# Two-of-eight experts: result rows stored by choice and token, and read back as plain blocks

## The chip, the cores and the metric

The kernel runs on one core of one Trainium2 chip. TensorE (PE in the rows, with PEld for its weight loads) multiplies, VectorE (DVE), ScalarE (ACT) and GpSimd (POOL) do the rest, and SyncE (SP) issues most of the transfers. The metric is the time of the whole program on the device in microseconds (us), median of several runs; lower is better.

## What is computed

Eight images of 16 x 16 tokens with 192 channels (2048 tokens) go through four layers, each an attention or convolution part and a feed-forward part. The change is at the seam between the third layer's experts and the fourth layer's attention:

```
def _L2_ffn_ref(hidden_states, router_w, w1, w2):
    ...
    probs = jax.nn.softmax(logits, axis=-1)
    topk_probs, topk_idx = jax.lax.top_k(probs, TOP_K)
    ...
    h = jnp.einsum('th,eih->tei', flat, w1)
    h = jax.nn.silu(h)
    outs = jnp.einsum('tei,ehi->teh', h, w2)
    sel = jnp.take_along_axis(outs, topk_idx[:, :, None], axis=1)
    combined = (sel * balanced[..., None]).sum(axis=1)
    ...
    t = t + _L2_ffn_ref(_ln_t(t), L2_ffn_router_w, L2_ffn_w1, L2_ffn_w2)
    t = t + _L3_attn_ref(_ln_t(t), L3_attn_w_qkv, L3_attn_w_proj)
```

Each token is sent to two of eight experts, the two results are weighted and added to the token, and the normalised sum is projected to the queries, keys and values of a full attention within each image.

## The kernel before, in words

The program is a row of stages, each a block in which every engine runs its own instruction list in order, with waits on semaphores between them; all engines meet at the end of a stage. Three stages matter here.

**Routing, `l2r` (function `route` with `top` = 2).** DVE finds each token's two experts and its place in a list of slots sorted by expert and padded to whole tiles of 128: SLOT_TILES = 40 tiles (5120 slots) for 4096 pairs of token and choice. A matrix product of two one-hot tables (OL and OHT) puts the token's number at its slot; an empty slot holds zero. DVE copies that table from PSUM to `token_at` (L2312), copies each token's two slot numbers to `slots` (L2315), and then works out the gates (from L2318 on). Meanwhile SP loads the experts' weights.

**The experts, `l2e` (`experts_any`).** The 40 tiles go in 20 pairs p. Per pair: POOL fetches the tokens' normalised rows from the DRAM buffer `xn` by `token_at` with two indirect transfers of 128 rows (L2428), up to four pairs ahead (RING = 4), waiting only for TensorE to have turned the pair that used the buffer; TensorE turns them (L2441 to L2443); DVE copies them to XT and copies the remaining weight rows of the tile's expert to W1R (L2506); TensorE does the first layer (L2452, L2455); ACT applies SiLU; TensorE turns the result, DVE copies it to HT (L2514), and TensorE does the second layer into `psY` (L2473). DVE copies that to Y (L2520, two buffers), and SP stores Y to the DRAM buffer `ys` in the order of the slots, 192 KB per pair (L2411). The order per slot of the loop is turn hidden of p+1, first layer of p+2, second layer of p, turn tokens of p+3.

**The attention's inputs, `l3p` (`combined_inputs`).** Image i has two tiles of 128 tokens. POOL gathers the two result rows of each token from `ys` by `slots`, four indirect transfers per image (L2734), those of image i+1 ahead of the statistics of image i. DVE adds them to X, weighted by the gates (combine, L2809, four instructions), takes mean and variance (L154, L157), POOL makes RSTD (L161 to L166), DVE normalises into xn (norm, L185), TensorE turns xn (L195), ACT copies it to xT (L203), TensorE multiplies to psQ and psK (L2759) and psV, ACT copies these to QF, KF (L2783) and Vall. Queries and keys are then split into three bf16 pieces: ACT makes the first and second (L255, L271), DVE the differences q_r and k_r (L267) and the third pieces (L279); SP stores them. DVE's order per image i:

```
norm(i + 1)
qp.vector(nc, dve, QF[u][:, :, :], i, u)
kp.vector(nc, dve, KF[u][:, :, :], i, u)
if i + 2 < B:
    combine(i + 2)
qp.third(nc, dve, i, u)
kp.third(nc, dve, i, u)
```

TensorE's order is Q(i), K(i), turn(i+1), V(i). ACT's is QF(i), first Q piece(i), KF(i), xT(i+1), first K piece(i), second Q piece(i), V(i), second K piece(i).

## Time and profile before

| what | value |
|---|---|
| median of 3 runs | 1279.95 us (1279.7 to 1282.09) |
| profiled execution, its own time | 1278.96 us |
| span of its trace, first to last instruction | 1277.1 us |
| mean granted TensorE clock, share of full | 0.885 |
| busy: PE, DVE, ACT, POOL | 82%, 46%, 34%, 22% |
| stage `l2e` in the trace | 735.2 to 901.8 us |
| stage `l3p` in the trace | 901.8 to 986.6 us |

The profiled execution's time is 1.9 us above its span, and 1.0 us below the median. Busy shares are means over the whole program: each stage has its own limit. In the rows, an entry in square brackets is how long the engine had been idle before the instruction and what it was then released by; POOL indirect transfers are called DMA_INDIRECT.

### The profile page before, as it was taken

What the parts mean: (1) busy time and instruction counts of PE and PEld (TensorE: products, weight loads), DVE (VectorE), ACT (ScalarE), POOL (GpSimd) and SP (SyncE); (2) the same over time, 40 slices, a digit from 0 to 9 for tenths busy, and PEclk for the clock granted to TensorE, in tenths of its full rate; (3) what the DMA queues carried; (4) which work ended last, traced back from release to release, by engine and by line L of the source; (5) the groups of instructions that cost most, each with busy time, mean ns of one, the idle gap of its engine ahead of it and who ended that gap; (6) DMA issues with size and microseconds to landing.
All of it is one profiled execution on the core that took longest, in us unless ns stands there. A gap on an engine that the chain in (4) does not pass through costs nothing. (4 is left out here: it accounts for less than half of the span.)

```text
span 1277.1 us, 21213 instructions
## 1 busy us (share of the span) xinstructions
PE 1045.2 (82%) x7522; PEld 794.2 (62%) x7523; DVE 591.8 (46%) x1420; ACT 435.0 (34%) x880; POOL 286.9 (22%) x473
## 2 busy tenths in 40 slices
PE   6795999996998887999898379999376898767890
PEld 5594878874656665787897336666255455465670
DVE  4742655543114555455655634444364677331112
ACT  3653255553323222344440011111054466412330
POOL 5454301102001111000013042220563212103104
PEclk9865999998999998899787589999698999958895
DMA  7444843300112000100003621120244432044534
GB/s 89 120 115 126 188 92 86 93 7 1 38 62 72 16 0 0 50 2 1 1 2 100 180 56 50 49 49 31 59 107 102 129 97 72 3 142 113 148 112 105
DMA packets 118625, 91.41 MB, mean 72 GB/s; under 512 B 33010, under 2 KB 110924, under 8 KB 117900
## 3 DMA queue, kind: packets, MB, share of 16 engines
q1 hardware_dynamic: 106935, 76.31, 23.1%
q0 software_dynamic: 4992, 10.23, 3.7%
q10 hardware_dynamic: 6613, 3.74, 1.1%
q8 instruction: 53, 0.87, 0.3%
q14 instruction: 32, 0.26, 0.1%
HBM read 64.38 MB, written 28.12 MB: 72 GB/s over the span
## 5 line engine op out<-in xcount | busy, mean ns | idle before, releaser
L1227 DVE TENSOR_REDUCE l0a_nmax<-l0a_psS 98x2 f32<-98x392 f32 x96 | 54.2, 566 | 54.1 <-PE l0a_psS L1042 50.1
L871 DVE TENSOR_REDUCE l3a_nmax<-l3a_psS 128x2 f32<-128x512 f32 x96 | 62.0, 686 | 33.7 <-PE l3a_psS L725 33.4
L2428 POOL DMA_INDIRECT l2e_X<-xn,token_at x40 | 38.4, 961 | 128.2 <-PE l2e_psX L2443 74.9
L2493 ACT ACTIVATE l2e_H<-l2e_psH 128x512 f32<-128x512 f32 x40 | 21.7, 595 | 131.2 <-PE l2e_psH L2455 131.2
L827 ACT ACTIVATE l3a_PT<-l3a_psST 128x512 f32<-128x512 f32 x96 | 54.7, 596 | 29.0 <-PE l3a_psST L755 28.4
L2473 PEld LDWEIGHTS l2e_psY<-W2T,l2e_HT 128*128 128x128 f32 x320 | 51.4, 190 | 18.3 <-issue 18.2
L1177 ACT ACTIVATE l0a_PT<-l0a_psST 98x392 f32<-98x392 f32 x96 | 47.2, 497 | 42.2 <-PE l0a_psST L1084 41.9
L2473 PE MATMUL l2e_psY<-W2T,l2e_HT 128*128 x320 | 57.3, 332 | 3.4 <-DVE l2e_HT L2514 2.1
L2452 PE MATMUL l2e_psH<-W1T,l2e_XT 128*128 x80 | 40.9, 635 | 2.8 <-issue 2.0
L2520 DVE COPY l2e_Y<-l2e_psY 128x384 f32<-128x384 f32 x20 | 11.1, 557 | 65.1 <-PE l2e_psY L2473 65.1
L725 PE MATMUL l3a_psS<-l3a_KS,l3a_QS 96*128 96x256 bf16 x192 | 37.3, 275 | 3.9 <-DMA l3a_KS<-kd 2.9
L2640 PE MATMUL l3e_psH<-l3e_XT,expert_W 128*128 128x256 f32 x96 | 30.3, 443 | 8.6 <-DMA expert_b<-in_L_ffn_b 7.3
L755 PE MATMUL l3a_psST<-l3a_QS,l3a_KS 99*128 99x256 bf16 x192 | 36.6, 273 | 0.4 <-ACT l3a_PT L827 0.3
L1403 DVE TENSOR_TENSOR X<-l0m_psY,X 128x384 f32<-128x384 f32 x8 | 4.5, 557 | 66.6 <-PE l0m_psY L1350 66.6
L2734 POOL DMA_INDIRECT l3p_Y<-ys,slots x32 | 31.8, 993 | 10.8 <-issue 10.5
L1350 PE MATMUL l0m_psY<-early,l0m_hT 128*128 128x192 f32 x192 | 32.3, 328 | 2.4 <-ACT l0m_hT L1375 2.4
L1350 PEld LDWEIGHTS l0m_psY<-early,l0m_hT 128*128 128x128 f32 x192 | 31.1, 190 | 3.9 <-ACT l0m_hT L1375 3.9
L1179 ACT ACTIVATE l0a_PT<-l0a_psST 120x360 f32<-120x360 f32 x48 | 22.1, 470 | 31.8 <-PE l0a_psST L1092 29.2
L1230 DVE TENSOR_REDUCE l0a_nmax<-l0a_psS 120x1 f32<-120x312 f32 x48 | 22.8, 479 | 20.6 <-PE l0a_psS L1051 19.0
L2653 PE MATMUL l3e_psY<-expert_W,l3e_HT 128*128 128x192 f32 x192 | 32.0, 327 | 0.0
L1041 PE MATMUL l0a_psS<-l0a_KS,l0a_QS 96*98 96x196 bf16 x144 | 31.8, 259 | 0.0
L2653 PEld LDWEIGHTS l3e_psY<-expert_W,l3e_HT 128*128 128x128 f32 x192 | 31.1, 190 | 0.3 <-issue 0.3
(534 smaller groups left out, 2752.6 us busy)
## 6 DMA issues: line engine op xcount, KB each, us to landing
l3a_QS<-qd SPq DMA_DIRECT2D x72, 64.0 KB, 2.2
l3a_KS<-kd SPq DMA_DIRECT2D x72, 64.0 KB, 2.2
expert_W<-in_L_ffn_w SPq DMA_DIRECT2D x8, 576.0 KB, 4.7
rd<-l0q_r_p SPq DMA_DIRECT2D x24, 168.0 KB
ys<-l2e_Y SPq DMA_DIRECT2D x20, 192.0 KB, 1.9
l0a_QS<-qd SPq DMA_DIRECT2D x54, 64.0 KB
l0a_KS<-kd SPq DMA_DIRECT2D x54, 64.0 KB
W2T<-in_w2t SPq DMA_DIRECT2D x2, 1536.0 KB
```

Source lines behind the costliest of these rows:

```text
L725: mm = nc.tensor.matmul(psS[item % 2][:, t * T:(t + 1) * T], QS[k % ring][0:SR, s, q:q + P], KS[k % ring][0:SR, s, u * T:(u + 1) * T], sta ...
L755: mm = nc.tensor.matmul(psST[item % 2][:, t * T:(t + 1) * T], KS[k % ring][:, s, key:key + P], QS[k % ring][:, s, u * T:(u + 1) * T], star ...
L827: nc.scalar.activation(PT[n % 3][:, s, :], psST[item % 2][:, :], ACT.Exp).then_inc(exp_done, 1)
L871: nc.vector.tensor_reduce(nmax[k % 2][:, TI * u:TI * (u + 1), s], psS[item % 2][:, :].rearrange("p (t k) -> p t k", t=TI), AX.X, ALU.max, ...
L1041: nc.tensor.matmul(o, q_[:, s, q], k_[:, s, keys], start=True, stop=False)
L1177: ex = nc.scalar.activation(PT[n % 3][0:WQ, s, :], psST[item % 2][0:WQ, 0:2 * W0], ACT.Exp)
L1227: mx = nc.vector.tensor_reduce(nmax[k % 2][0:WQ, 2 * j:2 * (j + 1), s], psS[item % 2][0:WQ, 0:2 * W0].rearrange("p (t k) -> p t k", t=2), ...
L1350: mm = nc.tensor.matmul(psY[a][:, t % 2 * C:(t % 2 + 1) * C], hT[p % 2][:, m, t * P:(t + 1) * P], Wd[:, m, :], start=(m == 0), stop=(m == ...
L2428: pool.indirect_dma_start(out=X[p % RING][:, t, :], out_offset=None, in_=G["xn"], in_offset=bass.IndirectOffsetOnAxis(ap=G["token_at"][:, ...
L2452: nc.tensor.matmul(psH[b][t][:, :], XT[b][:, t, :], W1T[:, 0, bass.ds(e * FI, FI)], start=True, stop=False)
L2473: mm = nc.tensor.matmul(psY[:, t * C:(t + 1) * C], HT[b][t][:, mb, :], W2T[:, bass.ds(e * NM + mb, 1), :].rearrange("p a c -> p (a c)"), s ...
L2653: mm = nc.tensor.matmul(psY[b][:, t * C:(t + 1) * C], HT[b][:, m, t * P:(t + 1) * P], W2[b][:, m, :], start=(m == 0), stop=(m == MF - 1))
```

## The change

The experts' results now go to DRAM by choice and token: row k * 2048 + token of `ys` holds the result of token for choice k. To get there the second one-hot table carries token - 2048 for the first choice and token + 1 for the second, so that sign and zero of the summed table tell first choice, second choice and empty slot apart. DVE works `token_at` and a second table `result_of` out of it; empty slots get a row number beyond the buffer. In `l2e` POOL, and no longer SP, stores each tile's rows with an indirect transfer by `result_of`, with a bound above which rows are dropped; a new semaphore `y_free`, raised by POOL once a pair's store has landed, tells DVE that a Y buffer is free. In `l3p` the rows of an image lie together, so SP loads them as 16 plain blocks of 128 x 2 x 192, all issued at the start of the stage; POOL gathers nothing there. In DVE's list for `l3p`, combine(i+2) moves ahead of the split of image i. The one-expert layer's routing uses the same table and gets a shifted copy in the place of the plain one.

```
@@ -2301,7 +2301,7 @@
-                    V.tensor_tensor(OHT[:].rearrange("p (k t) n -> p k t n", k=top), OH[:].rearrange("p (k t) n -> p k t n", k=top), free(token[:, 0:1], [0, top], [1, NT], [0, TILES]), ALU.mult).then_inc(hot_done, 1)
+                    V.tensor_tensor(OHT[:].rearrange("p (k t) n -> p k t n", k=top), OH[:].rearrange("p (k t) n -> p k t n", k=top), free(token[:, 0:1], [NT, top], [1, NT], [0, TILES]), ALU.mult).then_inc(hot_done, 1)
...
             dve.wait_ge(tab_mm, 1)
-            V.tensor_copy(G["token_at"][:, 0:TILES], psTab[:, 0:TILES]).then_inc(slots_done, 1)
+            tab = psTab[:, 0:TILES]
             if top == 2:
-                for k in range(2):
-                    V.tensor_copy(G["slots"][k][:, :], SI[:, k, :]).then_inc(slots_done, 1)
-
+
+                link(V.tensor_scalar(te[:, :], tab, 0.0, -1.0 - B * T, ALU.is_gt, ALU.mult))
+                link(V.tensor_tensor(te[:, :], tab, te[:, :], ALU.add))
+                V.tensor_scalar(G["token_at"][:, :], te[:, :], float(B * T), float(B * T - 1), ALU.add, ALU.min).then_inc(slots_done, 1)
+                link(V.tensor_scalar(late[:, :], tab, 0.0, None, ALU.is_gt))
+                link(V.tensor_scalar(empty[:, :], tab, 0.0, 2.0 * B * T, ALU.is_equal, ALU.mult))
+                link(V.tensor_tensor(empty[:, :], empty[:, :], late[:, :], ALU.subtract))
+                link(V.tensor_tensor(empty[:, :], tab, empty[:, :], ALU.add))
+                V.tensor_scalar(G["result_of"][:, :], empty[:, :], float(B * T), None, ALU.add).then_inc(slots_done, 1)
+            else:
+                V.tensor_scalar(G["token_at"][:, 0:TILES], tab, float(B * T), float(B * T - 1), ALU.add, ALU.min).then_inc(slots_done, 1)
+            if top == 2:
                 dve.wait_ge(imp_mm, 1)
...
@@ -2403,30 +2412,36 @@
 
         @block.sync
         def _(sp):
-            of_pair = lambda buf, p: image_of(buf.rearrange("(j n) c -> j (n c)", n=2 * P), p, 0, [C, P], [P * C, 2], [1, C])
-
-            def store(q, s):
-                p = q * RING + s
-                sp.wait_ge(y_done, p + 3)
-                sp.dma_start(of_pair(G["ys"], p), Y[s % 2][:, :, :]).then_inc(y_out[s % 2], 16)
-
             early.start(sp)
-            for b in range(2):
-                sp.sem_inc(y_out[b], 16)
-            with sp.Fori(0, PAIRS // RING) as q:
-                for s in range(RING):
-                    store(q, s)
             early.finish(sp)
-            for b in range(2):
-                sp.wait_ge(y_out[b], 16 * (PAIRS // 2 + 1))
 
         @block.gpsimd
         def _(pool):
-            for p in range(PAIRS):
+            at = lambda table, k: bass.IndirectOffsetOnAxis(ap=table[:, k:k + 1], axis=0)
+
+            def fetch(p):
                 pool.wait_ge(xt_mm, p + 1)
                 for t in range(2):
-                    pool.indirect_dma_start(out=X[p % RING][:, t, :], out_offset=None, in_=G["xn"],
-                                            in_offset=bass.IndirectOffsetOnAxis(ap=G["token_at"][:, 2 * p + t:2 * p + t + 1], axis=0)).then_inc(x_in[p % RING], 16)
+                    pool.indirect_dma_start(out=X[p % RING][:, t, :], out_offset=None, in_=G["xn"], in_offset=at(G["token_at"], 2 * p + t)).then_inc(x_in[p % RING], 16)
+
+            def put(p):
+                pool.wait_ge(y_done, p + 3)
+                for t in range(2):
+                    pool.indirect_dma_start(out=G["ys"], out_offset=at(G["result_of"], 2 * p + t), in_=Y[p % 2][:, t, :], in_offset=None,
+                                            bounds_check=2 * B * T - 1, oob_is_err=False).then_inc(y_out[p % 2], 16)
+
+            pool.sem_inc(y_free, 2)
+            for p in range(RING):
+                fetch(p)
+            for p in range(PAIRS):
+                if p + RING < PAIRS:
+                    fetch(p + RING)
+                if p:
+                    pool.wait_ge(y_out[(p - 1) % 2], 32 * ((p - 1) // 2 + 1))
+                    pool.sem_inc(y_free, 1)
+                put(p)
+            for b in range(2):
+                pool.wait_ge(y_out[b], 32 * (PAIRS // 2))
 
         @block.tensor
         def _(pe):
@@ -2516,7 +2531,7 @@
             def result_of(q, s):
                 p, b = q * RING + s, s % 2
                 dve.wait_ge(y_mm, p + 3)
-                dve.wait_ge(y_out[b], q * (RING // 2 * 16) + (s // 2 * 16 + 16))
+                dve.wait_ge(y_free, p + 1)
...
-        Y = [[st.sb(f"Y{t}{k}", [P, C]) for k in range(2)] for t in range(NT)]
+        Y = [[st.sb(f"Y{i}{k}", [P, TI, C]) for k in range(2)] for i in range(B)]
...
+            for i in range(B):
+                for k in range(2):
+                    sp.dma_start(Y[i][k][:], rows(G["ys"], (k * B + i) * T * C, [C, P], [P * C, TI], [1, C])).then_inc(y_in[i], 16)
             for i in range(B):
                 for pieces, dst in ((qp, G["qd"]), (kp, G["kd"])):
                     pieces.sync(sp, rows(dst, i // 2 * 3 * C * 2 * T + i % 2 * T, [2 * T, CH], [2 * C * T, 3], [2 * CH * T, 2], [1, T]), i, i % 2)
...
-            def gather(i):
-                for t in range(TI * i, TI * (i + 1)):
-                    for k in range(2):
-                        pool.indirect_dma_start(out=Y[t][k][:, :], out_offset=None, in_=G["ys"],
-                                                in_offset=bass.IndirectOffsetOnAxis(ap=G["slots"][k][:, t:t + 1], axis=0)).then_inc(y_in[t], 16)
-
             stats.init(pool)
-            gather(0)
             for i in range(B):
-                if i + 1 < B:
-                    gather(i + 1)
                 stats.gpsimd(nc, pool, i, i % 2)
...
-                            dve.wait_ge(y_in[t], 32)
+                            dve.wait_ge(y_in[i], 32)
                         else:
                             dve.wait_ge(added, 2 * TI * i + b + 1)
-                        nc.vector.scalar_tensor_tensor(G["X"][:, t, :], Y[t][k][:, :], G["gates"][k][:, t:t + 1], G["X"][:, t, :], ALU.mult, ALU.add).then_inc(added, 1)
+                        nc.vector.scalar_tensor_tensor(G["X"][:, t, :], Y[i][k][:, b, :], G["gates"][k][:, t:t + 1], G["X"][:, t, :], ALU.mult, ALU.add).then_inc(added, 1)
                 stats.vector(nc, dve, i, i % 2, (added, 2 * TI * (i + 1)))
 
             def norm(i):
@@ -2822,10 +2831,10 @@
                 u = i % 2
                 if i + 1 < B:
                     norm(i + 1)
+                if i + 2 < B:
+                    combine(i + 2)
                 qp.vector(nc, dve, QF[u][:, :, :], i, u)
                 kp.vector(nc, dve, KF[u][:, :, :], i, u)
-                if i + 2 < B:
-                    combine(i + 2)
                 qp.third(nc, dve, i, u)
                 kp.third(nc, dve, i, u)
...
-            "token": (np.arange(NT)[None, :] * P + np.arange(P)[:, None]).astype(np.float16), "blockones": head @ head.T,
+            "token": np.concatenate([np.arange(NT)[None, :] * P + np.arange(P)[:, None] + n for n in (-B * T, 1)], 1).astype(np.float16), "blockones": head @ head.T,
...
+        G["result_of"] = alloc("result_of", SLOT_TILES, U32)
-        slots = SLOT_TILES * P
-        G["ys"] = nc.dram_tensor("ys2", [slots, C], F32).ap()
+        G["ys"] = nc.dram_tensor("ys2", [2 * B * T, C], F32).ap()
```

On DVE at the end of the routing stage, the list around the copy of the slot table, before (te, late and empty are scratch rows of 40 numbers; imp begins the gates):

```order
L2310 CAST tile_expert<-l2r_te 128x40
L2312 CAST token_at<-l2r_psTab 128x40
L2315 CAST slots<-l2r_SI 128x16 x2
L2318 TENSOR_REDUCE l2r_imp<-l2r_psI 128x8
L2319 TENSOR_SCALAR l2r_bal<-l2r_imp 128x8
```

and now:

```order
L2310 CAST tile_expert<-l2r_te 128x40
L2315 TENSOR_SCALAR l2r_te<-l2r_psTab 128x40
L2316 TENSOR_TENSOR l2r_te<-l2r_psTab,l2r_te 128x40
L2317 TENSOR_SCALAR token_at<-l2r_te 128x40
L2318 TENSOR_SCALAR l2r_late<-l2r_psTab 128x40
L2319 TENSOR_SCALAR l2r_empty<-l2r_psTab 128x40
L2320 TENSOR_TENSOR l2r_empty<-l2r_empty,l2r_late 128x40
L2321 TENSOR_TENSOR l2r_empty<-l2r_psTab,l2r_empty 128x40
L2322 TENSOR_SCALAR result_of<-l2r_empty 128x40
L2327 TENSOR_REDUCE l2r_imp<-l2r_psI 128x8
```

Where three copies stood, eight instructions stand, seven of which depend on the one before or read the same table.

On POOL in the experts' stage, one piece of the difference (L2428 and L2425 fetch, L2430 stores):

```order
-L2428 DMA l2e_X<-xn,token_at 128x192 x40
+L2425 DMA l2e_X<-xn,token_at 128x192 x10
+L2430 DMA ys<-l2e_Y,result_of 4096x192 x2
+L2425 DMA l2e_X<-xn,token_at 128x192 x2
+L2430 DMA ys<-l2e_Y,result_of 4096x192 x2
+L2425 DMA l2e_X<-xn,token_at 128x192 x2
```

The forty fetches were one run ahead of the work; now five pairs are fetched first, and then the two stores of a pair stand between the fetches.

On DVE in the stage of the attention's inputs, one image of the loop before, from its norm on (l3p_xn is norm; l3p_q_r and l3p_k_r the differences; l3p_q_p and l3p_k_p the third pieces; X is combine, with its statistics behind it):

```order
L185 TENSOR_SCALAR l3p_xn<-X,MEAN,RSTD 128x192 x2
L267 TENSOR_TENSOR l3p_q_r<-l3p_QF,l3p_q_p 96x512
L267 TENSOR_TENSOR l3p_k_r<-l3p_KF,l3p_k_p 96x512
L2809 SCALAR_TENSOR_TENSOR X<-l3p_Y,gate,X 128x192 x4
L154 BN_STATS l3p_stat_part<-X 128x6 x2
L157 BN_AGGR l3p_stat_mv<-l3p_stat_part 128x2 x2
L279 TENSOR_TENSOR l3p_q_p<-l3p_q_r,l3p_q_p 96x512
L279 TENSOR_TENSOR l3p_k_p<-l3p_k_r,l3p_k_p 96x512
```

and the same image now:

```order
L185 TENSOR_SCALAR l3p_xn<-X,MEAN,RSTD 128x192 x2
L2818 SCALAR_TENSOR_TENSOR X<-l3p_Y,gate,X 128x192 x4
L154 BN_STATS l3p_stat_part<-X 128x6 x2
L157 BN_AGGR l3p_stat_mv<-l3p_stat_part 128x2 x2
L267 TENSOR_TENSOR l3p_q_r<-l3p_QF,l3p_q_p 96x512
L267 TENSOR_TENSOR l3p_k_r<-l3p_KF,l3p_k_p 96x512
L279 TENSOR_TENSOR l3p_q_p<-l3p_q_r,l3p_q_p 96x512
L279 TENSOR_TENSOR l3p_k_p<-l3p_k_r,l3p_k_p 96x512
```

Combine and its statistics now stand right behind norm, ahead of everything that waits for ACT.

## Rows read from the trace of the kernel before

**Rows 1.** Windows: busy PE, PEld, DVE, ACT, POOL, then clock, DMA share, GB/s.

```profile
735.20:901.80 166.60, 152.57 (x740) 99.24 (x740) 66.28 (x120) 22.99 (x41) 38.44 (x40) 0.97 0.18 48
901.80:916.25 14.45, 0.00 (x0) 0.00 (x0) 7.31 (x18) 0.00 (x0) 10.61 (x15) 0.50 0.20 57
933.11:973.25 40.14, 30.35 (x140) 23.79 (x140) 26.65 (x71) 21.48 (x40) 25.25 (x36) 0.91 0.45 114
```

**Rows 2.** Who waited for whom, 690 to 1000 us: total, times, longest.

```profile
PEld l2e_psH L2455 <- DVE l2e_W1R L2506: 13.0, 17, 0.8
```

**Rows 3.** Timeline and one window, end of routing: start, length, engine, line, operation.

```profile
729.86 0.18 DVE L2310 CAST tile_expert<-l2r_te 128x40 int32<-128x40 f32 x1
730.07 0.20 DVE L2312 CAST token_at<-l2r_psTab 128x40 uint32<-128x40 f32 x1
730.34 0.28 DVE L2318 TENSOR_REDUCE l2r_imp<-l2r_psI 128x8 f32<-128x128 f32 x1
724.00:726.00 2.00, 0.00 (x0) 0.00 (x0) 2.00 (x2) 0.00 (x0) 0.00 (x0) 0.50 0.00 0
```

**Rows 4.** Timeline, two slots of the experts' loop, with and without a fetch.

```profile
853.42 0.56 DVE L2520 COPY l2e_Y<-l2e_psY 128x384 f32<-128x384 f32 x1 [3.31 <-PE l2e_psY L2473]
...
855.49 0.95 POOL L2428 DMA_INDIRECT l2e_X<-xn,token_at  x1 [0.30 <-issue]
...
856.07 0.60 DVE L2506 COPY l2e_W1R<-W1T 64x512 f32 x1 [0.64 <-issue]
...
876.34 0.56 DVE L2520 COPY l2e_Y<-l2e_psY 128x384 f32<-128x384 f32 x1 [3.17 <-PE l2e_psY L2473]
...
878.88 0.42 DVE L2506 COPY l2e_W1R<-W1T 64x512 f32 x1 [0.47 <-issue]
```

**Rows 5.** Stores L2411, median us to landing; tile l2e_X, its fetches L2428.

```profile
ys<-l2e_Y SPq DMA_DIRECT2D x20, 192.0 KB, 1.9
...
DMA to landing us min/median/max: 2.5/2.7/4.2
```

**Rows 6.** Timeline, from the experts' last copies to the first norm.

```profile
894.92 0.56 DVE L2520 COPY l2e_Y<-l2e_psY 128x384 f32<-128x384 f32 x1 [1.82 <-PE l2e_psY L2473]
...
898.53 0.56 DVE L2520 COPY l2e_Y<-l2e_psY 128x384 f32<-128x384 f32 x1 [3.06 <-PE l2e_psY L2473]
901.88 0.10 POOL L148 MEMSET l3p_stat_exponent<- 128x2 f32 x1 [45.45 <-POOLq L77]
...
902.62 2.46 DVE L2817 MEMSET Vall<- 128x2880 f32 x1 [0.53 <-issue]
...
916.25 0.80 DVE L185 TENSOR_SCALAR l3p_xn<-X,MEAN,RSTD 128x192 f32<-128x192 f32 x2
```

**Rows 7.** Timeline, first image: its k_r, and the norm of image 2.

```profile
927.64 0.69 DVE L267 TENSOR_TENSOR l3p_k_r<-l3p_KF,l3p_k_p 96x512 f32<-96x512 f32 x1 [2.88 <-ACT l3p_k_p L255]
...
933.11 0.69 DVE L185 TENSOR_SCALAR l3p_xn<-X,MEAN,RSTD 128x192 f32<-128x192 f32 x2 [1.09 <-POOL RSTD L166]
```

**Rows 8.** Timeline, one later image, norm to norm.

```profile
949.17 0.69 DVE L185 TENSOR_SCALAR l3p_xn<-X,MEAN,RSTD 128x192 f32<-128x192 f32 x2 [1.09 <-POOL RSTD L166]
949.78 0.68 DVE L267 TENSOR_TENSOR l3p_q_r<-l3p_QF,l3p_q_p 96x512 f32<-96x512 f32 x1
951.73 0.69 DVE L267 TENSOR_TENSOR l3p_k_r<-l3p_KF,l3p_k_p 96x512 f32<-96x512 f32 x1 [1.28 <-ACT l3p_k_p L255]
952.34 1.39 DVE L2809 SCALAR_TENSOR_TENSOR X<-l3p_Y,gate,X 128x192 f32<-128x192 f32 x4
952.49 0.62 ACT L271 ACTIVATE l3p_k_p<-l3p_k_r 96x512 bf16<-96x512 f32 x1
954.86 0.65 DVE L279 TENSOR_TENSOR l3p_q_p<-l3p_q_r,l3p_q_p 96x512 bf16<-96x512 f32 x1
955.43 0.68 DVE L279 TENSOR_TENSOR l3p_k_p<-l3p_k_r,l3p_k_p 96x512 bf16<-96x512 f32 x1
957.20 0.70 DVE L185 TENSOR_SCALAR l3p_xn<-X,MEAN,RSTD 128x192 f32<-128x192 f32 x2 [1.09 <-POOL RSTD L166]
```

More of the change, by code:

```diff
@@ L2162, in route @@
         over, chosen = st.sb("over", [P, E, NT]), st.sb("chosen", [P, E, E])
-        te, te_cmp = small("te", SLOT_TILES), st.sb("te_cmp", [P, SLOT_TILES, E])
+        te, late, empty, te_cmp = small("te", SLOT_TILES), small("late", SLOT_TILES), small("empty", SLOT_TILES), st.sb("te_cmp", [P, SLOT_TILES, E])
         OH, OHT = (st.sb(n, [P, top * NT, TILES], F16) for n in ("OH", "OHT"))
@@ L2394, in experts_any @@
         y_out = [st.sem(f"y_out{b}") for b in range(2)]
-        xt_mm, xt_done, w_done, h_mm, h_done, ht_mm, ht_done, y_mm, y_done = st.sems("xt_mm xt_done w_done h_mm h_done ht_mm ht_done y_mm y_done")
+        xt_mm, xt_done, w_done, h_mm, h_done, ht_mm, ht_done, y_mm, y_done, y_free = st.sems("xt_mm xt_done w_done h_mm h_done ht_mm ht_done y_mm y_done y_free")
         early = Early(st, transfers)
@@ L2716, in combined_inputs @@
         psV = [st.ps(f"psV{u}") for u in range(2)]
-        y_in = [st.sem(f"y_in{t}") for t in range(NT)]
+        y_in = [st.sem(f"y_in{i}") for i in range(B)]
         added, pads_done, q_mm, q_free, k_mm, k_free, v_free = st.sems("added pads_done q_mm q_free k_mm k_free v_free")
@@ L2933, in __init__ @@
         self.sb(ctx, X=(P, NT, C), MEAN=(P, NT), RSTD=(P, NT), ident=(P, P), early0=(P, EARLY), early1=(P, EARLY))
-        for name, n, dt in (("tri", P, BF16), ("onesb", P, BF16), ("earlier", NT * E + E, BF16), ("count", P, I32), ("token", NT, F16)):
+        for name, n, dt in (("tri", P, BF16), ("onesb", P, BF16), ("earlier", NT * E + E, BF16), ("count", P, I32), ("token", 2 * NT, F16)):
             self.G[name] = ctx.enter_context(nc.sbuf_tensor(name, [P, n], dt))
```

## The prediction

> **What bounds the kernel now.** I read the page first (busy shares, the slices), then busy time by stage, then the list of waits around the change, then the timelines of the three stages. In the experts' stage TensorE works 152.57 us of 166.60 at a granted clock of 0.97 (nearly all at its upper level, 2.4 GHz), and POOL 38.44 [rows 1]: TensorE sets the pace, and what it still waits for is DVE's copy W1R, 17 times for 13.0 us in all [rows 2]. In the 14.45 us before the first norm of the attention's inputs TensorE does nothing at all [rows 1]: everyone waits for gathered rows. In the next stretch no engine is full: over the five images from norm 2 to norm 7, 40.14 us, TensorE has 30.35, DVE 26.65, POOL 25.25 [rows 1]. So one image takes 40.14 / 5 = 8.03 us there, and a loop of waits sets it, not an engine. [rows 8] show the loop: norm at 949.17; ACT must make xT before the first K piece, so k_r starts only at 951.73, after an idle 1.28; combine stands behind k_r and starts at 952.34; POOL's statistics end at 957.20, when the next norm starts after an idle 1.09. The combination, 4.86 us with its statistics (952.34 to 957.20), is in series with norm, turn and K piece.
>
> **The change, part by part.**
>
> Routing. From the copy of the table to the first row of the gates it was 0.27 us (730.07 to 730.34) [rows 3]. Now eight instructions on 128 x 40 stand there. The nearest pitch is that of two linked casts of this shape, 0.21 (729.86 to 730.07) [rows 3], and two of the eight don't wait for the one before: 6 x 0.21 + 2 x 0.15 = 1.6, so 1.3 more. Nothing covers it: no byte moves at 724 to 726 us [rows 3], so the weights are in, and the experts start when DVE is done. **+1.3** (1.0 to 1.6). The shifted copy for the one-expert layer is one instruction for one, 0.
>
> POOL in the experts' loop. The trace has no indirect store and none with a bound. The nearest row is the indirect fetch, 0.95 us and 0.30 between two [rows 4], pitch 1.25. A slot takes (876.34 - 853.42) / 3 = 7.64 us [rows 4], and two stores and two fetches take 5.0 of it: POOL has 2.6 us spare. The fetch of pair p+5 now waits behind the stores of pair p. They start when the copy of p has ended; two stores, two fetches and the landing are 1.25 x 4 + 2.7 [rows 4, 5] = 7.7 us later, and TensorE turns pair p+5 two slots later, at 15.3. So TensorE doesn't wait, and the slack of 7.6 us is the cover: nothing to pay unless a store takes 2.3 us or more. DVE's wait for a free Y (y_free) is for a store two slots old, also covered.
>
> DVE beside POOL. Where the second W1R copy meets a fetch it takes 0.60 in place of 0.42, and it ends 3.25 us after the start of the Y copy in place of 2.96 [rows 4]; as TensorE waits for it [rows 2], the slot is 0.29 longer. Stores and fetches now keep POOL busy for 5 us behind each Y copy, so more slots can meet this: between 0 and 17 x 0.29 = 4.9. Two of the four transfers lie where the fetch lay already, so I take **+1.0**. The Trainium skill, SBUF — State Buffer, section "SBUF: two separate sides", speaks against the change here: it says that a DMA issued from GpSimd needs the port pair that VectorE's fp32 copies within SBUF hold, that whoever comes second is blocked outright, and that issuing from SP avoids it; the copy's 0.60 fits the direction, and what the rule would cost if the whole instruction blocked is the fourth rival.
>
> End of the experts. The last copies start at 894.92 and 898.53 [rows 6] and take 0.56. Before, a plain store landed 1.9 us after issue [rows 5] and the next stage began at 901.88 [rows 6], 2.8 us after the last copy's end. Now the stores of pair 18 go out at about 895.6 and 896.9, and land by 899.6 (2.7, the fetches' median [rows 5]); POOL waits for that before it stores pair 19 at 899.6 and 900.9, which lands at 903.6 in place of some 901.2 (899.1, 0.2 to the issue, 1.9): **+2.4**. With the least plain landing, 1.9, it is +1.0; with the fetches' longest, 4.2 [rows 5], +5.4 (each 0.1 counts twice, as the last two pairs are in series). I take 2.7, as it is the same queue.
>
> Start of the attention's inputs. SP's first two blocks, each as large as a pair's store was, can go out at once and land about 2 us later [rows 5], at 904; DVE's fill of Vall, 902.62 + 2.46 = 905.08 [rows 6], hides them (if they took 1 us more than that, 0.5 would be seen). Then two combines of 2.52 (952.34 to 954.86 [rows 8]) end at 910.1; the first one's statistics are ready 4.86 after its start, at 909.9. The first norm comes at 910.1 in place of 916.25 [rows 6]: **-6.1**.
>
> The first image. From norm 0 to k_r it is 927.64 - 916.25 = 11.4 us [rows 6, 7], a chain through TensorE and ACT at the lower clock (0.50 up to norm 0 [rows 1]), which stays. Before, norm 2 came another 5.5 us later (933.11 [rows 7]), as combine followed k_r. Now combine 2 is over long before; after k_r come ACT's second K piece (0.62) and DVE's third (0.68) [rows 8]: 0.69 + 0.62 + 0.68 and handovers, 2.3 us. **-3.2**.
>
> Five later images. DVE's list is now norm 0.61, combine 2.52, q_r 0.68, k_r 0.69, then the wait for ACT's second K piece 0.62, and the third K piece 0.68 [rows 8]; the third Q piece lies in that wait. That is 5.8, with some 0.3 of handovers 6.1. The first K piece, ready 2.6 us after norm (951.73 against 949.17 [rows 8]), is hidden by combine, and so are the statistics (0.61 + 4.86 = 5.5, under 6.1). TensorE had 30.35 / 5 = 6.07 busy per image at a clock of 0.91 [rows 1], 5.5 at full clock: it fits, narrowly. 8.03 - 6.1 = 1.93 per image, five times: **-9.6** (period 5.6 to 7.0: -12.1 to -5.2). Images 6 and 7 have no combine behind them; from norm 7 on nothing changes.
>
> Sum: 1.3 + 1.0 + 2.4 - 6.1 - 3.2 - 9.6 = -14.2. From the profiled execution's 1278.96 us that gives 1264.8; the median of the runs is 1.0 above that execution, so **1266 us**. Less than 0.2% (2.6 us) can't be told from no change.
>
> **The rivals.**
>
> 1. The stores cost more than fetches: they land after 4.2 us (+5.4) and every slot meets the copy (+4.9): 1.3 + 4.9 + 5.4 - 18.9 = -7.3, 1272.5. For it: rows are written to scattered places, which no row shows. Against: 768 bytes a row before and now. Chance 0.15.
>
> 2. TensorE becomes the bound of the attention's inputs. An image needs 5.5 us of it at full clock, 11 at the 0.50 that it had before the first norm [rows 1]; at a mean of 0.75 the period is 7.4 and the five images give 3.1 in place of 9.6: 1272.5. For it: its share would be 90%. Against: a denser TensorE gave no fall of the clock in the experts' stage (0.97). Chance 0.07.
>
> 3. Slower: POOL becomes the pace of the experts. If a bounded indirect store takes 4 us of POOL, a pair needs 8.6 + 2.5 = 11.1 in place of 7.64, and 17 pairs lose 59 us: 1325. It costs from 2.3 us per store on and makes the whole change a loss from 2.7 (34 stores x 0.4 = 14). For it: nothing here shows a bound's price. Against: the fetch reads a table of row numbers too, and takes 0.95 [rows 4]. Chance 0.06.
>
> 4. W1R is blocked for whole transfers: 17 slots lose up to the 0.95 us of one [rows 4], 16 in place of 1: 1281, no change or slightly slower. This is the rule of the Trainium skill named above taken in full. Against: overlaps in this trace cost 0.29. Chance 0.05.
>
> 5. More is gained: stores land in 1.9 and meet nothing, and the period is 5.6 (DVE's busy 26.65 / 5 = 5.3 [rows 1] and handovers): 1.3 + 1.0 - 6.1 - 3.2 - 12.1 = -19.1, 1261. Chance 0.08.
>
> 6. The attention's inputs don't start earlier, because something else, such as the loads behind each other in SP's queue, comes as late as the gathers did, and the loop keeps its 8 us: within 2 us of before. Chance 0.04.
>
> **How the numbers follow.** The likeliest case, 0.55, is the sum; its own range is 1262 to 1270 (the bounds of routing, store landing and period, not all at one end). Cases 1, 2 and 5 lie at 1261 to 1272.5; a range of 1259 to 1274 holds them and leaves out 3, 4 and 6, 0.15. Faster by over 0.2%: 0.55 + 0.15 + 0.07 + 0.08 = 0.85. Within 0.2%: case 6 and half of 4, 0.06. Slower: case 3 and the other half of 4, with a little for a gain eaten by several costs, 0.09.
>
> **What would show it.** Routing: the gates' first row 1.6 us behind the table. POOL: stores at a pitch near 1.25, no wait of TensorE for fetched rows inside the loop; slots of 7.6 to 7.7. The end: 5 us instead of 2.8 from the last Y copy to the next stage. The first norm 8 to 9 us after that stage's start instead of 14.4; norm to norm 6.1 with no idle time for RSTD; combine right behind norm. I am wrong if slots grow beyond 8 us, if DVE still waits for blocks after its fill, or if norm to norm stays over 7.

## The result, and the profile after

The changed kernel takes 1271.32 us (median of 5 runs, 1269.5 to 1273.23) against 1279.95 (5 runs, 1278.24 to 1284.64) for the kernel before: ratio 0.9926, 95% interval 0.9903 to 0.9949, or 8.6 us less. The forecast was 1266 in a range of 1259 to 1274; the sum's own range, 1262 to 1270, does not hold the result. The profiled execution took 1272.05 us with a span of 1270.2, 6.9 less than the span before.

The windows of the changed kernel come first (busy PE, PEld, DVE, ACT, POOL, then clock, DMA share, GB/s). They are cut at the first and the last Y copy, the next stage's start, norm 0, norm 2 and norm 7:

```profile
764.85:900.64 135.79, 133.53 (x669) 89.55 (x667) 57.60 (x106) 18.45 (x34) 69.21 (x68) 1.00 0.16 45
900.64:913.90 13.26, 0.00 (x0) 0.00 (x0) 0.56 (x1) 0.00 (x0) 2.57 (x3) 0.60 0.01 0
913.90:922.56 8.66, 0.00 (x0) 0.00 (x0) 7.17 (x19) 0.00 (x0) 1.34 (x5) 0.50 0.86 264
922.56:935.22 12.66, 11.26 (x42) 8.29 (x43) 6.10 (x17) 5.01 (x10) 2.49 (x8) 0.68 0.23 68
935.22:964.95 29.73, 28.08 (x147) 22.05 (x145) 26.57 (x71) 21.69 (x41) 8.93 (x20) 1.00 0.39 100
```

The kernel before, cut at the same events where [rows 1] does not have the stretch:

```profile
735.50:761.24 25.74, 18.75 (x74) 9.71 (x74) 7.03 (x14) 4.36 (x7) 13.68 (x14) 0.82 0.20 54
761.24:898.53 137.29, 133.82 (x668) 89.53 (x666) 58.70 (x106) 18.45 (x34) 24.76 (x26) 1.00 0.17 46
898.53:901.88 3.35, 0.00 (x0) 0.00 (x0) 0.56 (x1) 0.00 (x0) 0.00 (x1) 1.00 0.17 59
916.25:933.11 16.86, 13.38 (x48) 9.41 (x48) 6.23 (x19) 6.63 (x12) 9.32 (x15) 0.72 0.21 54
```

The stretch to look at is 900.64 to 913.90: 13.26 us with 0.56 us of DVE, 2.57 of POOL, hardly any transfer, and nothing else. The stretch that answers to it took 3.35. The timeline of the changed kernel there (start, length, engine, line, operation, idle time before and its releaser):

```profile
900.26 0.98 POOL L2430 DMA_INDIRECT ys<-l2e_Y,result_of  x1 [0.30 <-issue]
...
900.64 0.56 DVE L2535 COPY l2e_Y<-l2e_psY 128x384 f32<-128x384 f32 x1 [3.06 <-PE l2e_psY L2488]
903.23 0.98 POOL L2430 DMA_INDIRECT ys<-l2e_Y,result_of  x1 [1.98 <-DMA ys<-l2e_Y,result_of]
904.52 0.98 POOL L2430 DMA_INDIRECT ys<-l2e_Y,result_of  x1 [0.30 <-issue]
913.68 0.91 SPq L2740 DMA_DIRECT2D l3p_Y<-ys  x2
913.92 0.22 DVE L2825 MEMSET Vall<- 128x192 f32 x1 [12.72 <-PEq L77]
913.94 0.10 POOL L148 MEMSET l3p_stat_exponent<- 128x2 f32 x1 [8.44 <-DMA ys<-l2e_Y,result_of]
```

The last store starts on POOL at 904.52, and stores by this table land a median of 2.4 us after their start, at most 2.7. That is 907.2 at the latest (by its own record this one landed at 906.60), yet the next stage begins at 913.9. The view puts POOL's 8.44 us down to the last store and DVE's 12.72 to line 77, where a stage's block ends. Between the two stands something that the views don't list: the records of the trace have a DRAIN of GpSimd at line 77, from 906.85 on, 6.60 us long, and the barrier of the stage right behind it at 913.45. Every stage ends with such a drain (the changed kernel has 14 at this line). In the kernel before, the record of the one in this stage begins at 854.02, just ahead of POOL's last two fetches (the last landed at 859.45), and ends at 861.13, 40 us ahead of the stage's end.

One image of the new loop on DVE, to be held against [rows 8]:

```profile
953.06 0.66 DVE L185 TENSOR_SCALAR l3p_xn<-X,MEAN,RSTD 128x192 f32<-128x192 f32 x2
...
953.64 1.40 DVE L2818 SCALAR_TENSOR_TENSOR X<-l3p_Y,gate,X 128x192 f32<-128x192 f32 x4
...
956.15 0.66 DVE L267 TENSOR_TENSOR l3p_q_r<-l3p_QF,l3p_q_p 96x512 f32<-96x512 f32 x1
...
956.73 0.68 DVE L267 TENSOR_TENSOR l3p_k_r<-l3p_KF,l3p_k_p 96x512 f32<-96x512 f32 x1
...
958.40 0.69 DVE L279 TENSOR_TENSOR l3p_k_p<-l3p_k_r,l3p_k_p 96x512 bf16<-96x512 f32 x1 [0.20 <-ACT l3p_k_p L271]
959.01 0.66 DVE L185 TENSOR_SCALAR l3p_xn<-X,MEAN,RSTD 128x192 f32<-128x192 f32 x2
```

Norm to norm is 5.95 us; the combination starts right behind norm, and the two waits of [rows 8], 1.28 for ACT and 1.09 for RSTD, are gone. TensorE is now busy 28.08 of 29.73 us at a clock of 1.00 (its upper level, 2.4 GHz). Who waited for whom in these 29.73 us (total, times, longest):

```profile
PE l3p_psT L195 <- DVE l3p_xn L185: 1.6, 3, 0.6
DVE l3p_k_p L279 <- ACT l3p_k_p L271: 1.0, 5, 0.2
```

TensorE still waits for DVE's norm, and DVE for next to nothing: DVE's list sets the pace, as forecast.

The routing's tail, DVE's rows of the changed kernel:

```profile
730.52 0.19 DVE L2310 CAST tile_expert<-l2r_te 128x40 int32<-128x40 f32 x1
730.74 0.20 DVE L2315 TENSOR_SCALAR l2r_te<-l2r_psTab 128x40 f32<-128x40 f32 x1
...
732.33 0.28 DVE L2327 TENSOR_REDUCE l2r_imp<-l2r_psI 128x8 f32<-128x128 f32 x1
```

Term by term, from these rows and those of before:

| term of the sum | forecast | measured |
|---|---|---|
| routing's tail: 1.59 (730.74 to 732.33) for 0.27 | +1.3 | +1.3 |
| experts' loop, first to last Y copy: 135.79 for 137.29 | +1.0 | -1.5 |
| last Y copy to the next stage: 13.30 (900.64 to 913.94) for 3.35 | +2.4 | +9.95 |
| stage's start to norm 0: 8.62 (913.94 to 922.56) for 14.37 | -6.1 | -5.75 |
| norm 0 to norm 2: 12.66 for 16.86 | -3.2 | -4.2 |
| five images: 29.73 for 40.14 | -9.6 | -10.4 |
| sum | -14.2 | -10.6 |

The spans differ by 6.9, so 3.7 us of the gain are missing elsewhere. From the first fetch to the first Y copy this execution took 27.27 us (737.58 to 764.85) and the one of before 25.74. The change need not be the reason: among the 14 profiles of this study the kernels with the old stores took 25.7 to 27.3 there, and those with the new ones 25.8 to 27.3. The rest is 0.66 ahead of the routing's tail (the cast of tile_expert at 730.52 in place of 729.86 [rows 3]) and 1.4 behind norm 7, where the change touches one instruction. Among the same profiles these two stretches spread over 5.9 and 8.9 us, with old stores and new, so a difference of this size in one pair of profiles says nothing about the change.

### The profile page after: what moved, and what is told of

It is laid out like the page before. It is cut to its first block and busy times, and to the rows that moved or that the text cites. A ratio compares the mean times of both kernels' runs of the same rounds, so it can differ in the third digit from the quotient of the medians.

```text
span 1270.2 us, 21210 instructions
## 1 busy us (share of the span) xinstructions
PE 1047.2 (82%) x7522; PEld 794.5 (63%) x7523; DVE 589.5 (46%) x1425; ACT 435.2 (34%) x880; POOL 296.7 (23%) x481
## 5 line engine op out<-in xcount | busy, mean ns | idle before, releaser
L2430 POOL DMA_INDIRECT ys<-l2e_Y,result_of x40 | 42.2, 1055 | 74.3 <-DVE l2e_Y L2535 64.3
L2425 POOL DMA_INDIRECT l2e_X<-xn,token_at x40 | 39.5, 988 | 59.0 <-PEq L2449 47.1
L767 PE MATMUL l3a_psO<-l3a_PT,Vall 128*32 128x256 f32 x384 | 31.6, 404 | 0.0
```

What stands on the lines that cost most here:

```text
L2425: pool.indirect_dma_start(out=X[p % RING][:, t, :], out_offset=None, in_=G["xn"], in_offset=at(G["token_at"], 2 * p + t)).then_inc(x_in[p ...
L2430: pool.indirect_dma_start(out=G["ys"], out_offset=at(G["result_of"], 2 * p + t), in_=Y[p % 2][:, t, :], in_offset=None, bounds_check=2 * B ...
```

## The experiments

The theory after the result: the attention's inputs gained what was forecast, and some 7 us of it went to the drain, which was hidden behind 40 us of the experts' loop before and now begins when POOL's last store has landed. Rival 1: the stores themselves are late. Rival 2: it is POOL's wait for one pair's landing ahead of the next pair's stores. Rival 3: the drain costs only right behind transfers.

**Without the drain.** The kernel leaves out GpSimd's drain at the end of the experts' stage, and clears the semaphores of POOL's transfers there after the next stage.

```diff
-        return self.ctx.enter_context(self.nc.Block())
+        return self.ctx.enter_context(self.nc.Block(**how))
...
-        block = st.block()
+        block = st.block(no_gpsimd_drain=True)
...
+        st.used += [s.num for s in G["held"]]
```

> The changed kernel, with the experts' stage closed without GpSimd's drain of its DMA queue (the semaphores of its transfers are cleared one stage later). Theory (the drain, 6.6 us behind the last store's landing, delays the next stage): from the last Y copy's start to the next stage's first POOL instruction some 6.7 us in place of 13.3, and the time is 6.6 us lower, about 1264.7. Rival 1 (the stores themselves, dropped rows or scattered writes, are late): still 13 us, 1271. Rival 2 (POOL's wait between the last two pairs of stores is most of it): still 11 us or more, 1270 to 1271.

Measured: 1263.04 us, ratio 0.985 (0.9825 to 0.9874). The timeline from the last stores to the next stage:

```profile
901.45 0.56 DVE L2534 COPY l2e_Y<-l2e_psY 128x384 f32<-128x384 f32 x1 [3.06 <-PE l2e_psY L2487]
904.05 0.98 POOL L2429 DMA_INDIRECT ys<-l2e_Y,result_of  x1 [1.99 <-DMA ys<-l2e_Y,result_of]
905.34 0.98 POOL L2429 DMA_INDIRECT ys<-l2e_Y,result_of  x1 [0.30 <-issue]
907.88 1.42 SPq L2740 DMA_DIRECT2D l3p_Y<-ys  x3
908.09 0.10 POOL L148 MEMSET l3p_stat_exponent<- 128x2 f32 x1 [1.77 <-POOLq L77]
```

The next stage begins 6.64 us after the last Y copy's start in place of 13.30. The stores, their landing and POOL's wait between the last two pairs (1.99) are all still there, so rivals 1 and 2 can't hold more than a part of these 6.64. The median is 8.3 us below the changed kernel's, of which 6.66 are at this place. The drain has not vanished: the records have it at the end of the next stage, from 958.20, 6.91 us long (POOL's last copy still runs in the first 0.3), where POOL is done early and it is hidden. It is as long there though the last transfer was 50 us old, which speaks against rival 3.

**The old kernel with a late POOL.** No transfer is added or changed.

```diff
             for p in range(PAIRS):
...
+            pool.wait_ge(y_done, PAIRS + 2)
```

> The kernel before, with one line more: POOL waits for the last Y copy ahead of the end of its program in the experts' stage. No transfer is added, stores stay plain and on SP. Theory (a drain of POOL's queue that was hidden and now begins when POOL's program ends): the drain begins at 899.1 us of the span in place of 854, ends 6.6 to 7.1 us later, and the next stage starts at about 906.1 in place of 901.9: 4.2 us more, about 1284. Rival 1 (the indirect stores are what is late): nothing moves, 1280. Rival 3 (the drain is long only right behind transfers): 0.3 us, hidden, 1280.

Measured: 1283.15 us, ratio 1.0015 (0.9996 to 1.0033): the time alone doesn't tell it from no change. The trace does:

```profile
900.58 0.56 DVE L2521 COPY l2e_Y<-l2e_psY 128x384 f32<-128x384 f32 x1 [3.06 <-PE l2e_psY L2474]
901.31 0.37 SPq L2411 DMA_DIRECT2D ys<-l2e_Y  x1
905.13 0.22 DVE L2817 MEMSET Vall<- 128x192 f32 x1 [3.99 <-PEq L77]
905.13 0.10 POOL L148 MEMSET l3p_stat_exponent<- 128x2 f32 x1 [46.66 <-remote]
```

The next stage comes 4.55 us after the last Y copy's start in place of 3.35. The drain was at the place the theory said, from 901.33, but 3.32 us long in place of 6.6 to 7.1. So the theory had the place right and the size wrong: 40 transfers cost 3.32, the changed kernel's 80 cost 6.60.

**Twice the fetches, no indirect store.** The kernel of the last run with each row tile fetched a second time into buffers that nobody reads.

```diff
+                twice(p)
+            pool.wait_ge(y_done, PAIRS + 2)
+            for b in range(2):
+                pool.wait_ge(d_in[b], 32 * (PAIRS // 2))
```

> The run in which POOL waits for the last Y copy, with each row tile fetched a second time into buffers that nobody reads: 80 transfers of POOL in the experts' stage in place of 40, all landed when the drain begins, and no indirect store. Theory (the drain costs about 0.083 us for each transfer that POOL queued in the stage, 3.32 us for 40): 6.6 us, the next stage 7.9 us after the last Y copy's start in place of 4.55: 3.3 us more than with 40, 1286.4. Rival 3b (the drain after the stores was longer because they were stores): 4.6 us and 1283. The second fetches can also meet W1R copies, up to 0.29 us a slot, which shows in the loop and not at its end.

Measured: 1286.96 us, ratio 1.0079 (1.0059 to 1.0099). The end of the stage:

```profile
899.45 0.56 DVE L2533 COPY l2e_Y<-l2e_psY 128x384 f32<-128x384 f32 x1 [3.06 <-PE l2e_psY L2486]
900.17 0.37 SPq L2413 DMA_DIRECT2D ys<-l2e_Y  x1
907.26 0.22 DVE L2829 MEMSET Vall<- 128x192 f32 x1 [7.26 <-PEq L77]
907.28 0.10 POOL L148 MEMSET l3p_stat_exponent<- 128x2 f32 x1 [47.45 <-remote]
```

7.83 us against a forecast of 7.9, and the drain's record is 6.59 long. The number of transfers counts, and not whether they fetch or store. The drains that began when all had landed, by the records:

| kernel and stage | transfers by POOL | drain, us |
|---|---|---|
| changed kernel, attention's inputs (POOL's last copy still runs) | 0 | 0.34 |
| kernel before, attention's inputs (the same) | 32 | 2.97 |
| late POOL, experts | 40 | 3.32 |
| changed kernel, experts | 80 | 6.60 |
| twice fetched, experts | 80 | 6.59 |
| without the drain, end of the attention's inputs (queued in the experts) | 80 | 6.91 |

From 40 to 80 it is 3.28 / 40 = 0.08 us for each transfer, and 40 such prices are nearly all of the 3.32: with no transfer and nothing running on POOL a drain of the changed kernel took 0.04 (at 690.88). Longer drains with few or no transfers are in the records too, but POOL was still at work in them: 2.78 us at 110.95 until a sum ended, 17.11 at 1250.77 with ten gathers still to go out. All transfers here are 128 rows of 768 bytes, so whether the drain counts transfers or their rows is not separated. The median of this run rose more than the end of the stage explains (some 9 us against 4.5); its profiled span rose by 4.5, and what the rest of the median is was not followed.

**Stores first, wait behind them**, alone and without the drain as well.

```diff
+                put(p)
                 if p:
                     pool.wait_ge(y_out[(p - 1) % 2], 32 * ((p - 1) // 2 + 1))
                     pool.sem_inc(y_free, 1)
-                put(p)
```

> The changed kernel with POOL's wait for the landing of pair p-1 moved behind the stores of pair p (the drain stays). Theory (two terms in series at the end: the wait between the last two pairs, and the drain): the stores of the last pair go out 2.0 us earlier, the drain stays 6.6 us, the next stage starts 11.3 us after the last Y copy's start in place of 13.3: 2.0 us less than the changed kernel, 1269.3. Rival (stores that overlap land later, or the drain then takes the time): 13.3 and 1271.

> The changed kernel with both: no drain at the end of the experts' stage, and the wait behind the stores. Theory: last Y copy to next stage 6.64 - 2.0 = 4.6 us; 2.0 us less than without the drain alone, 1261. Rival (the two are not in series): 6.6, 1263.

Measured: 1268.27 us (ratio 0.9921, 0.9903 to 0.9939) and 1259.14 us (0.987, 0.9846 to 0.9894). The end of the second:

```profile
899.45 0.56 DVE L2534 COPY l2e_Y<-l2e_psY 128x384 f32<-128x384 f32 x1 [3.06 <-PE l2e_psY L2487]
900.79 0.98 POOL L2429 DMA_INDIRECT ys<-l2e_Y,result_of  x1 [1.34 <-DVE l2e_Y L2534]
902.08 0.98 POOL L2429 DMA_INDIRECT ys<-l2e_Y,result_of  x1 [0.30 <-issue]
904.62 0.91 SPq L2740 DMA_DIRECT2D l3p_Y<-ys  x2
904.83 0.10 POOL L148 MEMSET l3p_stat_exponent<- 128x2 f32 x1 [1.77 <-POOLq L77]
```

5.38 us (899.45 to 904.83) in place of 6.64, a gain of 1.26 and not 2.0. POOL's first store follows the end of the copy (900.01) only 0.78 later, which the expectation had left out. With the drain it is 12.05 (895.31 to 907.36) in place of 13.30, 1.25: the two terms are in series. Together they give the lowest median of the study, and 0.987 against the changed kernel's 0.9926; that the two are faster than leaving out the drain alone (0.985, 0.9825 to 0.9874) shows at this place in the trace and not in the ratios.

**Its result rows made in the experts' stage.** On top of both.

```diff
-                link(V.tensor_scalar(late[:, :], tab, 0.0, None, ALU.is_gt))
...
-                V.tensor_scalar(G["result_of"][:, :], empty[:, :], float(B * T), None, ALU.add).then_inc(slots_done, 1)
+                V.tensor_copy(G["tab"][:, :], tab).then_inc(slots_done, 1)
```

> As the run with both, and the five instructions that make result_of moved from the routing to the head of DVE's list in the experts' stage, where DVE waits for the first rows (routing keeps one copy of the table in their place). Theory: routing's tail loses four of its instructions, 0.8 us, and the 1.1 us in the experts' stage are hidden: 1260.2. Rival (what DVE does there is not hidden, since the first W1R copies wait for it): 0.2 to 0.3 more than with both, 1261.3.

Measured: 1261.51 us, ratio 0.9871 (0.9851 to 0.9891), inconclusive beside 0.987. In the trace the routing's tail is 0.67 (731.91 to 732.58) in place of 1.59, 0.9 less against an expected 0.8. The five instructions end 5.8 us ahead of DVE's next one, so they are hidden. A gain of 0.9 us is below what these intervals can show.

**Order and loads apart.** The changed kernel with the old order (the diff), and the kernel before with the new order (the same lines the other way round).

```diff
+                qp.vector(nc, dve, QF[u][:, :, :], i, u)
+                kp.vector(nc, dve, KF[u][:, :, :], i, u)
                 if i + 2 < B:
                     combine(i + 2)
-                qp.vector(nc, dve, QF[u][:, :, :], i, u)
-                kp.vector(nc, dve, KF[u][:, :, :], i, u)
```

> The changed kernel with the combination back behind the K pieces; loads are plain blocks. Theory (the order on DVE gives the loop's gain, the loads give the stage's start alone): norm to norm 8.0 us in place of 5.95, norm 0 to norm 2 about 16.5 in place of 12.7, the start still 8.7: 10.3 + 4 us more than the changed kernel, about 1285.5. Rival (POOL without its gathers makes statistics ready earlier, and that gave the loop's gain): norm to norm 6 to 7, 1271 to 1277.

> The kernel before with the combination moved ahead of the pieces, and nothing else: rows are still gathered by POOL, the experts' stage is as before. Theory (order gives the loop's gain as far as gathers let it): four gathers of an image at a pitch of 1.25, their landing of 2.7 and a combination with statistics of 4.9 follow each other every second image, (5.0 + 2.7 + 4.9 + 0.7) / 2 = 6.6 us from norm to norm in place of 8.0; the start stays at 14.4; 5 x 1.4 and 2 to 4 us of the first image: 1269 to 1272. Rival (the loads give the gain): the loop keeps 8 us, 1279 to 1280. Were order alone enough: 6.0 us, 1266.

Measured: the loads with the old order 1285.35 us, ratio 1.0034 (1.0016 to 1.0051), 0.3% slower than before; the order alone 1271.24 us, 0.9936 (0.9915 to 0.9958), which can't be told from the whole change's 0.9926. What DVE waited for from norm 2 to norm 7, first with the new loads in the old order, then with the gathers in the new one:

```profile
DVE l3p_k_r L267 <- ACT l3p_k_p L255: 7.3, 5, 1.7
DVE l3p_xn L185 <- POOL RSTD L166: 6.5, 6, 1.1
```

```profile
DVE l3p_xn L185 <- POOL RSTD L166: 5.0, 4, 1.4
DVE l3p_k_p L279 <- ACT l3p_k_p L271: 1.0, 5, 0.2
```

With the old order and the new loads nothing of the loop is gained: five images take 40.91 us (40.14 before; the clock there was 0.79 against 0.91, and what that cost is not separated), and the start alone can't pay for the drain. With the order alone five images take 35.94, norm 0 to norm 2 12.48. There 7.2 us an image remain because POOL has four gathers (936.64 to 941.79 in one image) ahead of the statistics, and norm waits for RSTD. The expectation of 6.6 was 0.6 too low; it had priced that chain from single durations.

**The loop's 1.5 us.** Forecast was +1.0, for W1R copies that meet POOL. The copies of the kernel before and of the changed kernel (shortest, median, longest in ns):

```profile
L2506 DVE COPY l2e_W1R<-W1T x40: 418/425/669, 742.3 to 886.4; 64x512 f32 x40
```

```profile
L2521 DVE COPY l2e_W1R<-W1T x40: 418/422/425, 744.5 to 888.3; 64x512 f32 x40
```

In the kernel before 17 of the 40 took over 0.44 us; in the changed kernel none does. A first theory was that the fetches now go out behind the stores, when DVE has nothing to do. Two runs hold the old kernel's fetches back, to the Y copy and to the HT copies; one puts the changed kernel's fetches ahead of its stores. In the diff the wait for y_done is the first run's, the one for ht_done stands in its place in the second, and the last lines are the third's.

```diff
                 pool.wait_ge(xt_mm, p + 1)
+                if p > RING:
+                    pool.wait_ge(y_done, p - RING + 2)
...
+                    pool.wait_ge(ht_done, 2 * p - 6)
...
             for p in range(PAIRS):
+                pool.wait_ge(y_done, p + 3)
                 if p + RING < PAIRS:
                     fetch(p + RING)
```

> The kernel before with each fetch of POOL held back until the Y copy of the pair five before it has ended, so that it goes out where the changed kernel's POOL is busy; stores stay plain and on SP. Theory (the experts' loop became 1.5 us shorter because fetches no longer meet W1R's copies, not because of the stores): all 40 W1R copies 0.42 us, first to last Y copy 135.8 us in place of 137.3, slots of 7.46 to 7.71 in place of 7.46 to 7.92; the median 1.5 us lower, 1278.5, which the time alone can't tell. Rival (the plain stores of SP were what lengthened the slots): some copies stay at 0.60, the loop at 137.3.

> The kernel before with each fetch held back until the HT copies of the pair five before it have ended, some 4.5 us after the Y copy, where DVE has nothing to do until the next Y copy; in the run with fetches held back to the Y copy they still met DVE's loads of the expert's number and its W1R copies. Stores stay plain and on SP. Theory (fetches that meet DVE's work between the Y copy and the HT copies lengthen the slot; the changed kernel's fetches come behind its stores and so meet nothing): all W1R copies 0.42 us, slots 7.46 to 7.71, first to last Y copy 135.8 us in place of 137.3; about 1278.5. Rival (plain stores by SP lengthen the slots): 137.3 still.

> The changed kernel with each pair's fetches put ahead of its stores, both behind the Y copy: the fetches now meet DVE's loads and copies, the stores come when DVE has less to do. Theory: some W1R copies over 0.44 us again, first to last Y copy near 137.3 us in place of 135.8; the last stores come no later (no fetches are left there), the end as before; 1 to 1.5 us more than the changed kernel, 1272 to 1273. Rival (SP's plain stores were the reason): 135.8 and 1271.

Measured: 1279.65 us (0.9995, 0.9978 to 1.0011), 1278.99 (0.999, 0.9976 to 1.0004) and 1273.31 (0.9936, 0.9913 to 0.9959). Their loops, one window each, in this order:

```profile
763.54:900.80 137.26, 133.93 (x668) 89.53 (x666) 58.04 (x106) 18.46 (x34) 28.37 (x30) 1.00 0.17 49
```

```profile
758.86:895.69 136.83, 133.83 (x668) 89.52 (x666) 57.56 (x106) 18.45 (x34) 24.57 (x26) 1.00 0.16 46
```

```profile
765.14:900.83 135.69, 133.54 (x669) 89.55 (x667) 57.71 (x106) 18.45 (x34) 69.07 (x70) 1.00 0.17 47
```

With the fetches wholly out of the way all copies took 0.42 us, and the loop lost 0.46 of the 1.5, so stretched copies account for about a third of it. The third run did not bring them back: by the records 34 of its 40 copies lie beside a fetch, and none of these is stretched. It can't tell what stretched copies cost, but it shows that the loop of 135.7 does not need the fetches behind the stores. What the kernels with the longer loop have in common is SP's plain stores. The last run adds SP's plain stores to the changed kernel, to a buffer that nobody reads:

```diff
+                sp.wait_ge(y_done, p + 3)
+                sp.dma_start(of_pair(plain, p), Y[s % 2][:, :, :]).then_inc(z_out[s % 2], 16)
...
                 dve.wait_ge(y_free, p + 1)
+                dve.wait_ge(z_out[b], q * (RING // 2 * 16) + (s // 2 * 16 + 16))
```

> The changed kernel, in which SP also writes each Y pair with a plain store, as the kernel before did, to a buffer in DRAM that nobody reads (DVE waits for both). Open: of the 1.5 us by which the experts' loop became shorter, two runs gave only 0.5 to fetches that meet DVE's copies (136.8 us with the fetches out of the way, 135.7 with fetches back in the way). Theory now (SP's plain stores, which go out just behind the Y copy, slow DVE's loads of the expert's number and lengthen the slots by the other 1.0): first to last Y copy 136.8 to 137.3 us, half of the loads over 0.32 us; about 1272 to 1273. Rival (DVE's extra wait on SP's semaphore or something else of the old loop): the loop at 135.8 and one load in 40 over 0.32 us.

Measured: 1274.09 us, ratio 0.9959 (0.9935 to 0.9983). The loop:

```profile
765.71:905.66 139.95, 134.01 (x668) 89.52 (x666) 58.37 (x106) 18.45 (x34) 67.25 (x68) 1.00 0.24 71
```

The loop is 4.2 us longer, more than the 1.0 to 1.5 expected. By the records of DVE's register loads (the number of the expert, ahead of each W1R copy; the views don't list them) 18 of 40 took over 0.32 us before, 1 of 40 in the changed kernel, 17 of 40 here; the shortest take 0.30. All six profiles with SP's plain stores alone have 18, all seven without them 1; the 40 loads together took 14.2 to 14.5 us in the six and 12.4 to 12.5 in the seven, and the loops 136.8 to 137.7 and 135.7 to 135.8. So plain stores from SP just behind the Y copy go with slower loads of that number and longer slots. The difference of the loads, 1.8 us, could hold the 1.05 that are left; how much of the old loop's time it was is not measured by this run, as here each pair is written twice and DVE waits for both.

This run also has stretched copies again, though nearly all lie beside stores and not fetches:

```profile
L2537 DVE COPY l2e_W1R<-W1T x40: 418/422/489, 745.7 to 893.5; 64x512 f32 x40
862.66 0.49 DVE L2537 COPY l2e_W1R<-W1T 64x512 f32 x1 [0.59 <-issue]
862.69 1.00 POOL L2446 DMA_INDIRECT ys<-l2e_Y,result_of  x1 [0.30 <-issue]
```

By the records 15 of its 34 copies beside a store took over 0.44 us. What sets the stretched copies apart in the records is not the kind of transfer but when it starts. The 14 profiles have 97 copies over 0.44 us, 79 beside fetches and 18 beside stores; each time a transfer of POOL had started 0.51 to 0.76 us before the copy, or started within 0.03 us of it. Of the 463 other copies four have a transfer that started at such a time. In most slots of the changed kernel one store begins about 0.28 us before the first copy and the next 0.06 to 0.19 after the start of the second, so both miss.

## Why the prediction was right, and where it was not

The sign was right, and the attention's inputs gained what the prediction said and by the mechanism it gave. That the time lay in the range is in part luck: it comes out nearest to the first rival's 1272.5, whose reasons did not happen (stores landed in 2.1 to 2.7 us and not 4.2, no copy was stretched), because one term that was missing (+7.6 us at the end of the experts) was partly made up for by others that came out better than forecast (-2.5 in the loop, -1.5 in the attention's inputs). The step that failed is **End of the experts**, "+2.4 (1.0 to 5.4)", measured +9.95. It followed the stores to their landing and took that for the stage's end. What each engine does behind its last instruction was not in the sum, and neither were the 0.8 us from the copy to POOL's first store. The landing itself was well chosen (2.4 against 2.7). The drain, 6.60, is the missing term. It stood in the trace of before, hidden, and no view lists it; the nearest hint in the rows is [rows 6], where POOL's first instruction of the next stage is put down to "POOLq L77" and not to a transfer. Taking it away gave back 6.66 us at that place.

**Routing**, +1.3: right, from the pitch of linked instructions.

**DVE beside POOL**, +1.0: wrong in sign, -1.5. The step counted each transfer of POOL beside a W1R copy as a possible hit. In the changed kernel 34 of the 40 copies lie beside a store and none is stretched: in the slot at 855.92 a store of 1.01 us starts at 857.29, the W1R copy at 857.57, and it takes 0.42. The run with plain stores added has stretched copies beside stores, so it is a matter of when a store starts, which the number of transfers can't tell. Nor was the 0.29 us of a slot all the copy's: in [rows 4] the copy is 0.18 longer, and the idle time before it, where the expert's number is loaded, 0.17 (0.64 for 0.47). The rule of the Trainium skill (SBUF — State Buffer, section "SBUF: two separate sides"), the fourth rival, is not borne out here in its full size: most copies beside a transfer kept their 0.42 us, and the longest took 0.67. The stretched copies agree with its direction, and are worth the 0.46 us that the loop lost without them, no more.

**POOL in the loop**, 0: right. Stores take 0.98 to 1.24 us (median 1.01, for 0.98 of the fetches beside them), so no bound's price to speak of is seen, POOL has 69.21 busy of 135.79, and TensorE waits for no fetched row. So the third rival fell by far.

**Start, first image, five images**, -18.9: measured -20.35, as the steps said, norm to norm 5.95 for 6.1. Rival 2 (TensorE at half clock) did not come: 1.00 in this stretch. TensorE is 94% busy now, so no more than 1.65 us of these 29.73 are left to be had from DVE or POOL, though DVE's list still sets the pace. The prediction counted the three terms as the whole change's; the runs on order and loads show that they need both parts: the order gives 4.4 + 4.2 us by itself, loads by themselves next to nothing behind norm 0.

## What to carry to other kernels

A transfer that is moved to another queue takes with it what the stage's end does with that queue: look at what runs behind each engine's last instruction, also where it is hidden now, and ask when it will begin after the change. Where a stretch shows no engine busy and no byte moving, read the records that the views leave out before blaming the last transfer. Where a transfer meets another engine's copy, ask when each starts before counting how many can meet. And where a change has an order and a data path in it, time each alone: here moving two lines of order gave, within the noise, as much as the whole change.

## What was not expected of the hardware

- GpSimd's drain at a stage's end costs about 0.08 us for each DMA that POOL queued since the last one (0.04 us with none, 3.32 with 40, 6.60 with 80; all of 128 rows), fetch or store, even when all had landed some 40 us earlier.
- An indirect store with a bound takes POOL 0.98 to 1.24 us, about as an indirect fetch does (0.95 to 1.22), and lands in 2.1 to 2.7.
- A 64 x 512 fp32 copy on DVE beside an indirect transfer of POOL took 0.44 to 0.67 us in place of 0.42 only where the transfer had started 0.51 to 0.76 us earlier or within 0.03 us of it (97 copies in 14 profiles); why is open.
- Plain stores from SP of a buffer that DVE has just written go with slower register loads of DVE: 17 or 18 of 40 over 0.32 us, up to 0.58, and 1 of 40 without them; why stores from POOL don't is open.
